# A graph layer pair with routed experts: residual evictions on ScalarE, prep steps reordered, row tables without their fill

## The reference

```
x = x + gnn(LN(x));  x = x + moe(LN(x))
gnn: twice:  h = x @ W[l];  agg[d] = sum over edges s->d, and d->d, of dis[s]*dis[d]*h[s]
             x = relu(agg + b[l] + x @ resW + resb)          dis = 1/sqrt(degree + 1)
moe: router (256 -> 128 relu -> 6, softmax), the two best of six experts, softmax over the two;
     each expert is 256 -> 256 relu -> 256 relu -> 256 with biases; their weighted sum
```

## Time and profile before

| what | value |
|---|---|
| median of 3 runs | 1842.45 us (1842.28 to 1843.29) |
| the profiled execution | 1860.24 us, its span 1857.5 us |
| TensorE busy | 1779.8 us, 96% of the span |
| VectorE, ScalarE, GpSimd busy | 1036.7 (56%), 802.6 (43%), 340.4 us (18%) |
| mean granted clock of TensorE | 0.989 of full |
| moved by DMA | 416.81 MB, mean 224 GB/s |

### The profile page before, as it was taken

How to read it: one execution, slowest core, us unless ns; L and a number is a source line. 1 busy time by engine, 2 the same in 40 slices (tenths; PEclk the granted TensorE clock), 3 DMA queues, 4 the chain that set the end, 5 groups by cost and what they waited for, 6 DMA issues and landing times. The chain is left out here.

```text
span 1857.5 us, 41227 instructions
## 1 busy us (share of the span) xinstructions
PE 1779.8 (96%) x14272; PEld 1044.8 (56%) x14272; DVE 1036.7 (56%) x2813; ACT 802.6 (43%) x1822; POOL 340.4 (18%) x345
## 2 busy tenths in 40 slices
PE   4897999999999999999899999999999999899997
PEld 3675444444444444444444444444444478788886
DVE  7885655555555556555324444444444568555554
ACT  2467555555555555555312222222222232565553
POOL 1780000000000000000001111111111123333333
PEclk9999999999999999999999999999999999999999
DMA  7374999999898988899985555555554489323542
GB/s 222 102 133 63 334 291 319 313 319 265 269 299 260 308 249 281 318 359 337 352 318 185 184 184 184 187 186 184 184 184 184 182 261 331 94 88 112 140 135 78
DMA packets 135987, 416.81 MB, mean 224 GB/s; under 512 B 13685, under 2 KB 81611, under 8 KB 129640
## 3 DMA queue, kind: packets, MB, share of 16 engines
q1 hardware_dynamic: 90376, 255.13, 39.9%
q0 software_dynamic: 45392, 160.65, 29.6%
q10 hardware_dynamic: 144, 0.13, 0.0%
HBM read 162.27 MB, written 262.07 MB: 228 GB/s over the span
## 5 line engine op out<-in xcount | busy, mean ns | idle before, releaser
L1475 PE MATMUL bank<-parts,counts 128*128 128x512 f16 x4704 | 1078.9, 380 | 3.3 <-DVE counts L1590 3.3
L1475 PEld LDWEIGHTS bank<-parts,counts 128*128 128x128 f16 x4704 | 442.8, 98 | 509.0 <-issue 28.5
L1634 ACT ACTIVATE counts<-bank 128x392 f16<-128x392 f32 x768 | 336.5, 501 | 296.1 <-PE bank L631 296.1
L640 DVE TENSOR_TENSOR rows<-rows,iota_lo 128x2048 bf16<-128x2048 bf16 (+1 forms) x384 | 322.1, 890 | 20.3 <-PE bank L631 19.3
L631 PEld LDWEIGHTS bank<-rows 64*128 64x128 bf16 x6144 | 95.2, 94 | 82.1 <-issue 78.0
L467 POOL DMA_INDIRECT first_rows<-route_rows,route_spot_i x49 | 47.8, 976 | 498.7 <-DVE tokens L458 394.4
L2265 PE MATMUL bank<-y_t,counts 128*128 128x256 f32 x480 | 115.2, 383 | 5.7 <-ACT y_t L2337 5.1
L631 PE MATMUL bank<-rows 64*128 64x49 bf16 x6144 | 116.8, 185 | 0.1
L2265 PE MATMUL bank<-h_t,counts 128*128 128x256 f32 x480 | 113.7, 380 | 0.0
L2294 PE MATMUL bank<-counts,h_t 128*128 128x256 f32 x480 | 113.5, 380 | 0.0
L1490 ACT ACTIVATE middle<-bank 128x256 f32<-128x256 f32 x98 | 37.3, 381 | 175.9 <-PE bank L1475 161.7
(11 more groups left out here) (275 smaller groups left out, 1759.1 us busy)
## 6 DMA issues: line engine op xcount, KB each, us to landing
counts_table<-counts SPq DMA_DIRECT2D x25, 3136.0 KB, 15.3
counts<-counts_table SPq DMA_DIRECT2D x24, 3136.0 KB, 12.5
first_rows<-zero_rows POOLq DMA_DIRECT2D x3, 10530.0 KB, 59.7
second_rows<-zero_rows POOLq DMA_DIRECT2D x3, 10449.0 KB, 77.0
first_out<-zero_rows POOLq DMA_DIRECT2D x3, 10368.0 KB, 54.9
res_tile<-res_table SPq DMA_DIRECT2D x98, 128.0 KB, 2.8
first_rows<-zero_rows POOLq DMA_DIRECT2D x1, 10270.0 KB, 58.7
second_rows<-zero_rows POOLq DMA_DIRECT2D x1, 10191.0 KB, 68.6
```

Of the source, the lines that this page charges most:

```text
L640: return nc.vector.tensor_tensor(rows, k, v, ALU.is_equal)
L1475: mm = nc.tensor.matmul(acc[:, 0:2 * dim], counts[:, b, s, o * P:(o + 1) * P], parts[:, s, :], start=s == 0, stop=s == tiles - 1)
L1634: nc.scalar.activation(counts[:, b, :, quad_nodes(q)], bank[4 + q % 4][:, 0:RUN * tiles].rearrange("p (n s) -> p s n", s=tiles), ACT.Copy) ...
```

## The change

1. Prep: the residual evictions of tiles 0 to 39 go from VectorE to ScalarE (`Copy` with a scale per row), those of tiles 40 to 48 stay on VectorE. The bias is no longer added there; `add_bias` adds it in the pair stage, once per tile, in VectorE's queue ahead of `add_res`, in place on `res_tile`. The inverses are steps of their own.
2. Prep: the packing is one copy by ScalarE of `dst` into the upper 16 bits of each `src` word, after tile 3 (the shift is 16 instead of 14). VectorE's statistics, histogram, starts, norms, disorders and the first key batch come ahead of its residual evictions; the key batches 1 to 4 stand behind the message tiles 1, 11, 21 and 31; the one-hots, roots, scales and the flag are put at other tiles.
3. Tables: no fill. `store_fillers` writes 256 rows at each expert's region in each table (6 transfers, 4.7 MB in all), and an expert's rows begin behind them (`region_base` + 256). A last block ends at the expert's last row and starts 256 rows ahead of it; the rows that it shares with the block before it, or the fillers, are cast out by `skips` at its head. The lists' ends are computed in `final_list`, before the lists are announced; `block_ends` is gone.
4. In the fallback for unsorted edges (not run here) some semaphores are merged.

```diff
-        HIST_BEFORE = (None, 1, 2, 3, 4, 5, 6)
-        OFFSETS_BEFORE = 8
-        NORMS_BEFORE = 20
-        STATS_AFTER = (16, 20, 25, 31)
-        KEYS_AFTER_RES = (29, 39)
-        KEYS_AFTER_H = (9, 17, 27)
-        FLAG_AFTER_H = 33
+        HIST_BEFORE = (None, 1, 5, 7, 10, 14, 16)
+        OFFSETS_BEFORE = 18
+        NORMS_BEFORE = 22
+        KEYS_AFTER_RES = (44,)
+        LATE_RES = 40
+        PACK_AT = 3
+        ROOTS_AT = 44
+        ROOTS_AFTER_H = (7, 17, 27, 37)
+        SCALE_AFTER_H = (8, 18, 28, 38)
+        KEYS_AFTER_H = (5, 15, 26, 37)
+        FLAG_AFTER_H = 42
-        ONEHOTS_AFTER_H = (6, 14, 16, 24, 27, 30, 33, 36)
+        ONEHOTS_AFTER_H = (7, 9, 17, 19, 27, 29, 37, 40)
...
+                def residual(t):                                   # ScalarE, tiles 0 to 39, after turned_copy(t + 2)
+                    act.wait_ge(products_ready, t + 1)
+                    act.wait_ge(rstd_ready, group_of(t) + 1)
+                    nc.scalar.activation(res_rows[:, t, :], res_bank(t)[:, 0:dim], ACT.Copy, scale=rstd[:, t:t + 1]).then_inc(res_ready, 1)
+                def pack():                                        # ScalarE, after tile PACK_AT
+                    act.wait_ge(dst_loaded, 16 * 3)
+                    act.wait_ge(src_loaded, 16 * 4)
+                    nc.scalar.activation(src_sb[:, :].bitcast(U16).rearrange("p (c h) -> p c h", h=2)[:, :, 1], dst_sb[:, 0:cols], ACT.Copy).then_inc(packed_ready, 1)
...
                 stats(1)
+                inverse(0)
                 head_onehots(2)
                 head_onehots(3)
+                stats(2)
+                inverse(1)
+                head_onehots(4)
+                stats(3)
+                inverse(2)
+                head_onehots(5)
+                head_onehots(6)
+                inverse(3)
+                stats(4)
+                offsets()
+                stats(5)
+                inverse(4)
+                starts()
                 ... (the bias sums)
+                stats(6)
+                inverse(5)
+                stats(7)
+                inverse(6)
+                norms()
+                stats(8)
+                inverse(7)
+                disorders()
+                inverse(8)
+                for step in range(6):
+                    key_step(0, step)
+                residual(LATE_RES)
+                residual(LATE_RES + 1)
+                residual(LATE_RES + 2)
+                scale(0)
+                for t in range(LATE_RES + 3, tiles):
                     residual(t)
...
+                    n, step = divmod(t - 1, BATCH)
+                    if 0 <= step < 6 and n + 1 < batches:
+                        key_step(n + 1, step)
-                    if t == 40:
+                    if t == 46:
                         flag_and_bounds()
...
+    def add_bias(self, dve, T, o, u):
+        dve.wait_ge(self.res_back[o], u * 16 + 16)
+        self.nc.vector.tensor_tensor(self.res_tile[:, o, :], self.res_tile[:, o, :], self.bias_sum[:, 0, :], ALU.add).then_inc(self.res_biased, 1)
...
                         if there(i * 2 - 3):
+                            if r == 0:
+                                update.add_bias(dve, i * 2 - 3, 1, i - 2)
...
                         if there(i * 2 - 2):
+                            if r == 2:
+                                update.add_bias(dve, i * 2 - 2, 0, i - 1)
...
-        def store_zeros(pool):
-            stored = 0
-            for table in (first_rows, second_rows, first_out):
-                cols_of = table.shape[1]
-                for lo in range(0, per_part, quarter):
-                    hi = min(lo + quarter, per_part)
-                    pool.dma_start(table.rearrange("(p r) d -> p r d", p=P)[:, lo:hi, :], ...)
-                    stored += 16
-                    pool.wait_ge(zeros_stored, stored)
+        def store_fillers(pool):
+            for table in (first_rows, second_rows, first_out):
+                cols_of = table.shape[1]
+                for h in range(2):
+                    pool.dma_start(table.rearrange("(e r) d -> e r d", e=experts)[:, h * P:(h + 1) * P, :].rearrange("e p d -> p e d"), ...)
...
+                    link(nc.vector.scalar_tensor_tensor(block_end[:, :], block_end[:, :], -float(ROWS), block_row[:, :], ALU.add, ALU.min))
+                    link(nc.vector.tensor_tensor(skips[:, n:], block_row[:, n:], block_end[:, n:], ALU.subtract))
+                    link(nc.vector.tensor_scalar(block_row[:, :], block_end[:, :], 0.0, None, ALU.max))
```

More of the change, by code:

```diff
@@ L86, in __init__ @@
         self.res_back = [sem(f"res_back{l}_{o}") for o in range(2)]
+        self.res_biased = None if last else sem(f"res_biased{l}")
         self.sum_ready = sem(f"sum_ready{l}")
@@ L129, in add_res @@
         dve.wait_ge(self.sums_out, T + 1)
-        dve.wait_ge(self.res_back[o], u * 16 + 16)
+        if self.last:
+            dve.wait_ge(self.res_back[o], u * 16 + 16)
+        else:
+            dve.wait_ge(self.res_biased, T + 1)
         if later:
@@ L500, in gnn_moe_kernel @@
     region = (-(-nodes // ROWS) + 1) * ROWS
-    idle = NB - -(-nodes // ROWS)
-    table_rows = experts * region + idle * ROWS
+    table_rows = experts * region
     EARLY = pairs - 4
@@ L775, in keys_after_h @@
             return next(((n + len(KEYS_AFTER_RES)) * BATCH // 2 + t - a for n, a in enumerate(KEYS_AFTER_H) if a <= t < a + BATCH // 2), None)
-        ROOTS = [("rows", g) for g in range(8)] + [("nodes", 0), ("rows", 8)] + [("nodes", n) for n in range(1, batches)]
+        ROOTS = [("rows", g) for g in range(9)] + [("nodes", n) for n in range(batches)]
         def res_bank(t):
@@ L945, in _ @@
                     turned_copy(t)
+                    if 2 <= t < LATE_RES + 2:
+                        residual(t - 2)
+                    if t == PACK_AT:
+                        pack()
                     if t == 16:
@@ L1252, in _ @@
-                for t in range(6, 13):
-                    residual(t)
[L1254 to L1268, removed]
-                    if t == 40:
-                        scale(0)
@@ L1283, in _ @@
+                    if t in SCALE_AFTER_H:
+                        scale(1 + SCALE_AFTER_H.index(t))
+                    if t == 39:
                         overflow()
@@ L1339, in _ @@
                 def _(act):
-                    act.wait_ge(degree_ready, 1)
-                    nc.scalar.activation(true_dis[:, :], degree[:, :], ACT.Sqrt, bias=1.0).then_inc(root_ready, 1)
+                    act.wait_ge(stage_done, DEGREES_MADE)
+                    nc.scalar.activation(true_dis[:, :], degree[:, :], ACT.Sqrt, bias=1.0).then_inc(stage_done, 1)
                 @block.vector
@@ L1626, in vector @@
                 for T, kept in ((tiles - 2, None), (tiles - 1, parts[:, tiles - 1, :])):
+                    update.add_bias(dve, T, T % 2, T // 2)
                     sums(T // 2, T % 2)
@@ L2031, in _ @@
                     work.final_list(dve)
-                    work.block_ends(dve)
                     work.first_normal(dve)
@@ L2111, in expert_blocks @@
             block_end = sb("block_end", [P, 2 * NB], F32)
-            ends = sb("ends", [P, 2 * NB], F32)
+            skips = sb("skips", [P, 2 * NB], F32)
             block_table = sb("block_table", [P, 2, 2 * NB], I32)
@@ L2656, in tile @@
                         dve.sem_inc(update.sums_out, 1)
+                        update.add_bias(dve, T, o, u)
                         update.add_res(dve, T, o, u)
```

126 lines of the change are left out of this document (44 added, 82 removed).

## The result

The changed kernel takes 1832.85 us (median of 4 runs, 1831.58 to 1834.06), the kernel before 1842.87 beside it (4 runs, 1842.28 to 1846.48): ratio 0.9928, 95% interval [0.9906, 0.995]. It is faster by 10.0 us; forecast were 30.4 (1812, range 1802 to 1826). On two other chips it took 1829.87 against 1846.18 and 1830.42 against 1846.16 (0.9917 [0.9901, 0.9933] and 0.9914 [0.9895, 0.9933]), so that 16 us is the better figure: the intervals overlap, and the kernel before varies more (1839.8 to 1854.2 over all its runs but the first profiled one, 1860.24) than the changed one (1828.0 to 1834.8).

A forecast was written before the change was run, and what follows sets the result against it. TensorE bounds the full pair stage, so gains lie in its holes in prep, turn and experts. Prep -19.5, turn -11.5 and experts +0.6 sum to -30.4 us on 1860.24; less 1.0%, 1812 (own range 1806 to 1819, full 1802 to 1826).

The forecast's parts named there:

- step 6: Turn to the second layer: without the fill, 9.0 us of wait and 2.4 of low clock go, -11.5 (bounds -11.5 and -3).
- the last line of the sum: Whole kernel: -30.4 us on the profiled 1860.24, then 1.0% taken off because that execution exceeds the median: 1812.
- Step 1 and 3: Prep's residual phase: with ScalarE's evictions at 1.2 us a tile it ends near 87.5 instead of 111.5, -24 (-20 to -28).
- Rival A: Residual phase: ScalarE becomes the bound at 1.7 us a tile, phase ends near 105, time 1826; chance 0.14.
- Step 2: VectorE's order up to the starts in prep: fetches begin within 1 us of 50.44, the last still issues near 114.
- Step 4: Prep's message phase: later keys and flag give back 4.5 us (0 to +9); prep ends near 165, gain 19.5 (11 to 28).
- the floor: Prep's end: if the block's end waits for POOL's expert copies to land, near 161, only the best cases are cut off.
- Step 5: Pair stage: the fill leaves and one `add_bias` per tile enters VectorE's queue, cost 0 (0 to +2).
- Rival C: Pair stage: `add_bias` stops the count builds if even loads land later than 22.3 us; 1865 at 24.5; chance 0.04.
- rival B: Turn: the counts store, at 15.3 us, holds the first load of `parts`, so the wait stays; 1820; chance 0.10.
- Step 7: Experts: moved list ends make TensorE wait about 2 us before block 14, mostly lost in a later hole; +0.6 (0 to +2.7).

The follow-up runs named there:

- before_tables: Kernel before with only the tables' part (small fillers instead of the fill, list ends moved): 1846.24 and 1846.15 us against 1846.18 and 1847.05.
- after_flag: Changed kernel with the flag and bounds at message tile 43 instead of 46: 1831.95 us.
- after_flag42: Changed kernel with the flag and bounds behind message tile 42 instead of 46: 1831.38 us, against 1847.44 for the kernel before.
- after_fill: Changed kernel with the full fill of all three tables put back (12 transfers): 1844.57 us, 0.9985 of the kernel before.
- after_again: Changed kernel, unchanged, profiled a second time and run for five more rounds: 1829.87 us.
- after_fill8: Changed kernel with the full fill put back for two of three tables (8 of 12 transfers): 1833.07 us, 0.9917 of the kernel before.

## Why the prediction missed

The mechanisms were mostly right; what failed was step 6, which counted 11.5 us of the turn that ordinary executions don't lose (0 measured in their median), and behind it the last line of the sum, where one profiled execution, 1.0% above the median, was scaled as a whole. A second term was too large: prep, 15.7 us instead of 19.5.

*Step 1 and 3, ScalarE's evictions.* The end of the residual phase came at 87.50 as forecast, but not by the forecast's working. Timeline of ACT of the changed kernel:

```profile
75.78 0.48 ACT L922 ACTIVATE parts<-bank,rstd 128x256 f32<-128x256 f32 x1
76.13 0.52 ACT L907 ACTIVATE counts<-counts,row_mean 128x256 f32<-128x256 f32 x1
76.53 0.39 ACT L917 ACTIVATE counts<-bank 128x256 f32<-128x256 f32 x1
76.79 0.49 ACT L922 ACTIVATE parts<-bank,rstd 128x256 f32<-128x256 f32 x1
```

The three take 1.01 us a tile here, and TensorE runs at its own 1.09, not at the 1.2 assumed. That the end fits is in part luck: the working left out eight matmuls of 3.60 us (line 1066, at 53.31) in the same stretch, which made up for the quicker tiles. Tile 44 was held as named: VectorE evicts tile 40 at 80.62. Rival A is refuted. Groups of instructions, 0 to 90 us (busy us, mean ns, idle before them):

```profile
L922 ACT ACTIVATE parts<-bank,rstd 128x256 f32<-128x256 f32 x40 | 19.1, 477 | 0.9 <-DVE rstd L1122 0.9
L1128 DVE TENSOR_SCALAR parts<-bank,rstd 128x256 f32<-128x256 f32 x9 | 4.3, 483 | 2.7 <-PE bank L1017 1.9 <-DVE parts L1128 0.5
```

ScalarE does the scaled eviction in 477 ns, VectorE in 483. The rule of the Trainium skill that multiplies belong on VectorE ("ScalarE: Activation LUTs", Rules for kernel authors) finds no difference to rest on in this case; its budget gave an estimated 0.51 us.

*Step 2.* First fetch at 51.87 (forecast within 1 us of 50.44, so 0.4 outside), last at 116.47 (114). Right enough.

*Step 4, message phase.* The first pair matmul came at 168.65, not 165 to 166. The flag cost about what was said, 3.5 us on the path against 3. The term that was mis-sized is the floor: the expert copies do land near 161, as estimated (161.3 to 164.1), but the block's end comes 4.2 us behind, at 165.5 to 168.3. With one trace of before (185.31) the gain is 16.7 against 19.5 forecast; the work itself ended 18.9 us sooner (ScalarE at 183.99 and 165.07), and 2.3 went to that end. The rest is mostly the first trace's own prep, 2.4 us longer than the mean that follows. With four traces of before, two of before_tables (182.20, 182.97; the same prep) and five with the changed prep and its drain (165.85 to 168.65, after_flag and after_flag42 left out), the means are 182.9 and 167.2: 15.7.

*Step 5.* Right: pair stage 737.8 us against 737.5, 49 more additions of 418 ns each (of line 130) without cost, and `res_tile` loads at 4.2 us in the median instead of 11.8. Rival C is refuted.

*Step 6, the turn.* The step that failed. In the two traces it gave its 11.5 us almost to the letter (9.12 of wait, 2.27 of clock), and rival B is refuted for them: without the fill the counts store landed in 9.2 us instead of the 15.3 that the rival assumed, and the first load of `parts` at 905.3, 2.1 us before TensorE began. But in three of four profiled executions of the kernel before there was nothing to win: the wait belongs to an execution whose fill ran 30 us late. I had the sign of it: 17.8 us between the profiled execution and the median, against 11.5 us in one wait whose releaser, a 10 MB transfer, had no fixed time. They had to be set against each other. Instead the 1.0% was spread over everything.

*Step 7, experts.* Forecast +0.6 (0 to +2.7). From the turn's first matmul to the last matmul's end: 909.7, 910.8 and 910.6 us in the traces of before without the wait, and 913.5, 911.2 and 911.9 in the three of the changed kernel: about +1.8. Inside the bounds, but not shown to be the lists' doing: before_tables has the same lists and took 910.8 and 910.1, and the other traces of changed kernels without a wait at the turn spread from 909.9 to 914.5. The wait of 2.77 at 1546 is as forecast (about 2); the hole behind it shrank more than forecast, 2.50 here against 5.08.

*The sum again.* Prep -15.7, turn 0, experts +1.8, pairs -0.5 (738.7 us from first pair matmul to the turn's, against 739.2): -14.4. The medians of the spans of ordinary runs are 1842.1 and 1842.8 before and 1827.4 and 1827.2 after, 15 apart. So the 30.4 lost 11.5 to the turn and 3.8 to prep. What the trace can't show is whether the wait stands in some of the ordinary runs, too; before_tables, without a fill on two chips, says that it is worth nothing in the median.

The fill's removal is still no idle part of the change. With prep shortened and the fill kept, the wait stood in the trace and the kernel was 14.7 us slower. Why the fill took 748 us there and 721 to 725 in three traces of before isn't settled; had it taken 721, it would have landed at 888, ahead of the loads. Two causes stand untested side by side: the changed prep, and the tables' new layout (312 rows a partition instead of 322), which after_fill keeps. Nor does the trace of after_fill cover the whole 14.7: its wait and low clock are 10.5 of the 13.1 us by which its span exceeds after_again's.

## What to carry to other kernels

Before a profile is used as a budget, set its own time against the ordinary runs: if it is 1% above, look for a wait of that size whose releaser is a large transfer without a due time, and take a second profile or put that term at a chance. Two parts of a change can be worth next to nothing each (0 and 1.6 us) and 16 us together; try them apart and together. When an engine's last work moves ahead at the end of a block, ask what else the block's end waits for: here GpSimd's outstanding transfers, 2 us at first, 5.5 once the flag was out of the way (7.03 against 1.50).

## What the runs showed that was not expected

- A block's end with GpSimd's drain let the next stage begin 4.2 us behind the landing of GpSimd's last copy, at 165.5 to 168.3 us. Without the drain it began 1.5 us behind the last work. What the 4.2 us are made of, no run shows.
- The fill shares the engines with SP's loads rather than holding them up: seven loads of 0.9 MB land in 22.5 us in the median beside it, in 11.3 without, and the first of them, issued at 912.05, landed 20.8 us later, ahead of the fill (939.5). The Trainium skill says so of two queues ("DMA: Bandwidth & Descriptors", Queues, rings and completion order: packet by packet); the trace agrees.
- The time outside the span differs between kernels: 4.5 us in the median of 29 runs of the kernel before, 1.7 for before_tables, 2.3 and 3.6 for the changed kernel. It doesn't follow the fill alone: 3.5 for after_fill with all of it, 1.7 for after_fill8 with two thirds. The spans of before_tables are 1 to 2.6 us longer than those of the kernel before (1844.7 and 1844.2 against 1842.1 and 1843.0). So the 0 of before_tables is a sum of the two. Neither was followed up.
- TensorE stood 3.5 and 4.0 us near 156 us in two profiles of the kernel before, released by nothing that the profile shows, and 0.8 to 3.7 near 148 with the changed prep; the other two profiles of the kernel before had 0.56 and none, before_tables 1.77 in one trace and none in the other. It is a part of prep's spread, and its cause is open.
